# A fourth pair of each batch row by seven products, in a kernel of gated experts and an adapted linear layer on one core

## The reference, cut to what matters

```python
# layer 0, x is (8, 512, 256): 8 batch rows of 512 tokens
w, sel = top_k(softmax(cond_8), 2)               # two experts for each batch row, weights normalised
for each expert e:
    acc += w_e * (gelu(x @ gate_e) * (x @ up_e)) @ down_e      # 256 -> 1024 -> 256
x = x + acc + (gelu(x @ shared_gate) * (x @ shared_up)) @ shared_down
# layer 1, a linear layer with a low-rank part that depends on the batch row
x = x + x @ W_base.T + b_base + 2 * sum_e cond_8[b, e] * (x @ A_e.T) @ B_e.T
```

## Time and profile before

| what | value |
|---|---|
| median of 3 runs | 800.66 us (800.28 to 801.05) |
| the profiled execution, its own time | 800.03 us |
| its span, first to last instruction | 798.2 us |
| what lies outside the span | 1.8 us |
| busy share of the span: PE, PEld, DVE, ACT, POOL | 99%, 85%, 85%, 59%, 36% |
| granted PE clock | 0.999 of full speed |
| one batch row of the second stage | 67.58 us |

### The profile page before, as it was taken

The page is one execution under the profiler, slowest core; times in us unless marked ns, Lnnn a source line. Parts: engine busy times, 40 slices in busy tenths (PEclk is TensorE's granted clock), DMA queues, the critical chain, the costliest instruction groups (busy, mean ns, idle before and its releaser), DMA issues.

```text
span 798.2 us, 13016 instructions
## 1 busy us (share of the span) xinstructions
PE 792.9 (99%) x4014; PEld 678.4 (85%) x4014; DVE 676.6 (85%) x874; ACT 470.1 (59%) x715; POOL 290.5 (36%) x266
## 2 busy tenths in 40 slices
PE   9999999999999999999999999999999999999998
PEld 7888888888888888889888889888888888898887
DVE  4886987987876898899789789988978988998986
ACT  6564564564654656576566566566656655656653
POOL 1440321321110662552255055344415615533420
PEclk9999999999999999999999999999999999999999
DMA  7340520302313442353353254335334323533300
GB/s 211 75 120 12 148 80 12 121 1 89 110 40 80 139 135 84 106 154 112 102 152 90 87 163 121 106 105 131 105 120 146 105 80 122 152 107 103 84 1 28
DMA packets 120143, 80.56 MB, mean 101 GB/s; under 512 B 62481, under 2 KB 115473, under 8 KB 120081
## 3 DMA queue, kind: packets, MB, share of 16 engines
q1 hardware_dynamic: 120080, 79.88, 34.2%
HBM read 67.28 MB, written 12.58 MB: 100 GB/s over the span
## 4 chain that ended last, share of the span: by engine, by line
PE 99%; DMA 1%; DVE 0%; ACT 0%; SPq 0%; DVEq 0%; issue 0%
PE ps_ring L736 62%; PE ps_acc L736 36%; DMA raw<-_L_cond_shared_gate_dram 1%; PE ps_acc L944 0%; PE ps_acc L964 0%; PE ps_ring L754 0%; DVE stage L1798 0%; PE ps_ring L758 0%; PE ps_ring L762 0%; PE ps_acc L850 0%; PE ps_ring L964 0%; ACT xc L1065 0%; PE ps_acc L990 0%; ACT wide L1065 0%; SPq L456 0%
## 5 line engine op out<-in xcount | busy, mean ns | idle before, releaser
L736 PE MATMUL ps_ring<-xc,wide 128*128 128x512 f32 (+1 forms) x2076 | 454.1, 367 | 0.0
L736 PEld LDWEIGHTS ps_ring<-xc,wide 128*128 128x128 f32 x2076 | 366.3, 188 | 65.5 <-issue 0.3
L1065 ACT CAST inner_hi<-post 128x512 fp32r<-128x512 f32 x192 | 117.9, 621 | 140.8 <-DVE post L1723 67.6
L1404 DVE TENSOR_TENSOR inner_lo<-post,inner_hi 128x512 fp32r<-128x512 f32 x192 | 162.1, 858 | 12.2 <-ACT inner_hi L1065 11.8
L736 PE MATMUL ps_acc<-inner_hi,wide 128*128 128x512 f32 x504 | 172.0, 390 | 0.0
L1068 ACT ACTIVATE post<-ps_ring 128x512 f32<-128x512 f32 (+1 forms) x132 | 73.3, 558 | 89.4 <-PE ps_ring L736 85.4
L736 PEld LDWEIGHTS ps_acc<-inner_hi,wide 128*128 128x128 f32 x504 | 94.7, 188 | 19.2
L695 POOL TENSOR_TENSOR post<-post 128x256 f32<-128x256 f32 x48 | 34.5, 741 | 187.7 <-DVE post L1671 187.7
L736 PE MATMUL ps_acc<-inner_lo,wide 128*128 128x512 f32 x252 | 98.3, 390 | 0.0
L1723 DVE SCALAR_TENSOR_TENSOR post<-post,coef_now,ps_ring 128x512 f32<-128x512 f32 x80 | 59.4, 742 | 30.7 <-PE ps_ring L736 25.4
L736 PE MATMUL ps_acc<-inner_hi,sh_dn 128*128 128x512 f32 x256 | 83.8, 389 | 0.0
(11 more groups left out here) (122 smaller groups left out, 863.0 us busy)
## 6 DMA issues: line engine op xcount, KB each, us to landing
raw<-n_L_cond_skill_gate_dram SPq DMA_DIRECT2D x32, 256.0 KB, 2.9
raw<-in_L_cond_skill_up_dram SPq DMA_DIRECT2D x32, 256.0 KB, 3.4
raw<-n_L_cond_skill_down_dram SPq DMA_DIRECT2D x32, 256.0 KB, 3.7
xbuf<-n_L_cond_skill_gate_dram SPq DMA_DIRECT2D x32, 256.0 KB, 2.9
xbuf<-in_L_cond_skill_up_dram SPq DMA_DIRECT2D x32, 256.0 KB, 3.3
xbuf<-n_L_cond_skill_down_dram SPq DMA_DIRECT2D x32, 256.0 KB, 3.7
xt_scratch<-xbuf SPq DMA_DIRECT2D x8, 512.0 KB, 3.2
sh_scratch<-stage SPq DMA_DIRECT2D x8, 512.0 KB, 2.8
```

The lines of the kernel that those rows point to most:

```text
L736: last = pe.matmul(dst, left_[a], right_[b], start=start and n == 0, stop=stop and n == len(PASSES) - 1, skip_group_check=adds)
L1065: return nc.scalar.copy(dst, src)
L1404: return V.tensor_tensor(dst, src, hi.bitcast(F32), ALU.subtract)
```

## The change

- `SEVEN` becomes [1, 3, 5, 7]; batch row 0 keeps 3, 5, 7 (`FIRST_SEVEN`). So step 2 of batch rows 1 to 7 is by seven products too, behind only steps 0 and 1.
- The splits move: DVE and ACT take pair 9 (the next row's pair 1) at step 14, pair 2 at step 1, pair 3 and, with layer 1, pair 4 at step 4, and nothing at steps 0 and 2. The sums of pair 1 are split at step 0, those of pair 3 at `L1_STEP`.
- `L1_STEP` goes from 3 to 4. `layer1_sum` and `layer1_hi` stay at step 1, `layer1_lo` comes behind DVE's seven-product work of step 2, `turn_output` stands at step 5 behind the multiplication.
- `FOLD_STEP` 9 to 8; DVE's addition for it from step 12 to 9, its splits from step 13 to 12; `bw` from step 5 to 0.
- The token sums of batch row b+1 go to a second place in `sh_dn` for odd rows and are split at step 13 of row b; before, at step 3 of row b+1.
- x1 is written over `base`. The transfer of `base` for row b therefore waits for `x1_ready` (x1 split) instead of `x1_done`.
- POOL's order in a later row was: sums of pair 3, base plus x, `ex_c22`, sums of pair 5, token sums, `ex_c22`, sums of pair 7, `ex_c22`. It becomes the list in the diff.

```diff
-    L1_STEP = 3
+    L1_STEP = 4
-    FOLD_STEP = 9
-    W_EFF_STEP = 12
+    FOLD_STEP = 8
+    W_EFF_STEP = 9
+    W_EFF_LO_STEP = 12
     X_STEP = 8
+    T_STEP = 13
-    SEVEN = [3, 5, 7]
+    SEVEN = [1, 3, 5, 7]
+    FIRST_SEVEN = SEVEN[1:]
...
-        def sums_x(hl):
-            return xc[1][:, hl * 1024:(hl + 1) * 1024]
+        def sums_x(par, hl):
+
+            if par == 0:
+                return xc[1][:, hl * 1024:(hl + 1) * 1024]
+            return sh_dn[:, 2048 + hl * 1024:2048 + (hl + 1) * 1024]
...
-        x1 = post[:, 0:2 * S]
+
+        x1 = base
...
-        SPLIT_FIRST = {0: 2, 2: 3, 5: 4, 6: 5, 9: 6, 10: 7, 13: 8}
-        SPLIT_LATER = {0: 1, 2: 2, 5: 4, 6: 5, 9: 6, 10: 7, 13: 8}
-        SUMS_FIRST = {4: 0, 8: 1, 12: 2}
-        SUMS_LATER = {8: 1, 12: 2}
+        SPLIT_FIRST = {0: 2, 2: 3, 5: 4, 6: 5, 9: 6, 10: 7, 13: 8, 14: 9}
+        SPLIT_LATER = {1: 2, 4: 3, 6: 5, 9: 6, 10: 7, 13: 8, 14: 9}
+        SUMS_FIRST = {4: 1, 8: 2, 12: 3}
+        SUMS_LATER = {0: 0, 8: 2, 12: 3}
...
-                    sp.wait_ge(x1_done, b * 2)
+                    sp.wait_ge(x1_ready, b)
                     sp.wait_ge(sh_stored, 16 * B)
                     sp.dma_start(base, sh_dram[b]).then_inc(base_landed, 16)
...
+            def row(b, first, last):
+                if first:
+
+                    pool.wait_ge(sh_stored, 16 * B)
+                    sums_of_x(0)
+                    sums_of_weights(b, 1)
+                    row_sum(b)
+                    ex_c22(b, 1)
+                    sums_of_weights(b, 2)
+                else:
+                    sums_of_weights(b, 1)
+                    ex_c22(b, 0)
+                    row_sum(b)
+                    sums_of_weights(b, 2)
+                    ex_c22(b, 1)
                 if not last:
 
                     if not first:
                         pool.wait_ge(out_landed, b * 128)
                     pool.wait_ge(ex_t_ready, b + 1)
                     sums_of_x(b + 1)
-                ex_c22(b, 1)
-                sums_of_weights(b, 2)
+                sums_of_weights(b, 3)
                 ex_c22(b, 2)
+                if not last:
+                    sums_of_weights(b + 1, 0)
+                ex_c22(b, 3)
...
                         if k % 2 == 0:
-                            seven_products(b, par, k, SEVEN.index(k // 2))
-                            down(b, k - 2)
-                            down(b, k - 1)
+                            seven_products(b, par, k, SEVEN.index(k // 2), first)
+                            if k == 2:
+
+                                pe.wait_ge(x1_done, b * 2)
+                            down(b, k - 2, first)
+                            down(b, k - 1, first)
...
                     if k == L1_STEP and not first:
-                        split_pair(SEVEN[0])
-                        split_sums_w(b, 0)
-                    if k == L1_STEP + 1 and not first:
+                        split_sums_w(b, 1)
+                        split_pair(4)
                         add_bias(b - 1)
...
                             ex_seven(b, par, k, SEVEN.index(k // 2))
                             if k in split_at:
                                 split_pair(split_at[k])
+                            if k == 2:
+                                layer1_lo(b - 1)
...
-                    if k == 1 and not first:
-                        layer1_lo(b - 1)
                     if first and k == 1:
                         acc1_to_stage(Q - 1)
                     if k == L1_STEP and not first:
-                        split_pair(SEVEN[0])
-                        split_sums_w(b, 0)
-                    if k == L1_STEP + 1 and not first:
-                        turn_output(b - 1)
+                        split_sums_w(b, 1)
+                        split_pair(4)
                     if k == CONST_STEP and first:
                         layer1_constants()
+                    if k == T_STEP and not last:
+                        split_sums_x(b + 1, 1 - par)
```

More of the change, by code:

```diff
@@ L379, in cond_resid_kernel, with sevens_of, seventh, whole @@
         LAST_PARTS = [(c, slice(h * S // 2, (h + 1) * S // 2)) for c in range(2) for h in range(2)]
-        SPLIT_FIRST = {0: 2, 2: 3, 5: 4, 6: 5, 9: 6, 10: 7, 13: 8}
-        SPLIT_LATER = {0: 1, 2: 2, 5: 4, 6: 5, 9: 6, 10: 7, 13: 8}
-        SUMS_FIRST = {4: 0, 8: 1, 12: 2}
-        SUMS_LATER = {8: 1, 12: 2}
[L387 to L397, removed]
+        SPLIT_FIRST = {0: 2, 2: 3, 5: 4, 6: 5, 9: 6, 10: 7, 13: 8, 14: 9}
+        SPLIT_LATER = {1: 2, 4: 3, 6: 5, 9: 6, 10: 7, 13: 8, 14: 9}
+        SUMS_FIRST = {4: 1, 8: 2, 12: 3}
+        SUMS_LATER = {0: 0, 8: 2, 12: 3}
+        def sevens_of(first):
+            return FIRST_SEVEN if first else SEVEN
+        def seventh(b, k, first):
+            return sum(2 * pr < k for pr in sevens_of(first)) + (0 if first else b * NS - 1)
+        def whole(b, k, first):
+            now = k - 2 * sum(2 * pr < k for pr in sevens_of(first))
+            return now if first else b * (K - 2 * NS) + 2 + now
+        def seven_no(b, n_s):
+            return b * NS + n_s - 1
         block = ctx.enter_context(nc.Block())
@@ L696, in ex_c22, with row_sum @@
                 last.then_inc(ex_c22_done, 1)
[L698 to L706, removed]
+            def row_sum(b):
                 pool.wait_ge(base_landed, b * 16 + 16)
@@ L906, in seven_products, with down_chunk, down @@
                     last.then_inc(ex_product, 1)
[L908 to L913, removed]
+            def down_chunk(k, first):
+                return 1 - k % 2 if k // 2 in sevens_of(first) else k % 2
+            def down(b, k, first):
+                j, p = k % IC // 2, down_chunk(k, first)
                 pe.wait_ge(inner_ready, b * K + k + 1)
@@ L943, in one @@
                 def one(m, k, hl_w, hl_x):
-                    return pe.matmul(ps_acc[m][:], ex_dn(hl_w, k % IC // 2, down_chunk(k), m), inner_s[hl_x][:, k % 4, :],
+                    return pe.matmul(ps_acc[m][:], ex_dn(hl_w, k % IC // 2, down_chunk(k, False), m), inner_s[hl_x][:, k % 4, :],
                                      start=False, stop=k == K - 1 and (hl_w, hl_x) == (0, 1))
@@ L1015, in row @@
                     elif k >= 2:
-                        pe.wait_ge(gelu_done, whole(b, k - 1))
+                        pe.wait_ge(gelu_done, whole(b, k - 1, first))
                     elif k == 0:
@@ L1024, in row @@
                     elif k >= 2:
-                        pe.wait_ge(mul_done, whole(b, k - 1))
+                        pe.wait_ge(mul_done, whole(b, k - 1, first))
                     else:
@@ L1330, in row @@
                 for k in range(K):
-                    if k // 2 in SEVEN:
+                    if k // 2 in sevens_of(first):
                         if k % 2 == 0:
@@ L1365, in row @@
                             .then_inc(bw_hi, 1)
-                    act.wait_ge(mul_done, whole(b, k) + 1)
+                    act.wait_ge(mul_done, whole(b, k, first) + 1)
                     if k >= 4 or not first:
@@ L1709, in row @@
                                 split_pair(split_at[k])
+                            if k == 2:
+                                layer1_lo(b - 1)
                         continue
-                    dve.wait_ge(gelu_done, whole(b, k) + 1)
-                    dve.wait_ge(up_done, whole(b, k) + 1)
-                    if k % 2 == 0 and (k // 2 - 1 in SEVEN or (k == 0 and not first)):
+                    dve.wait_ge(gelu_done, whole(b, k, first) + 1)
+                    dve.wait_ge(up_done, whole(b, k, first) + 1)
+                    if k % 2 == 0 and (k // 2 - 1 in sevens_of(first) or (k == 0 and not first)):
                         dve.wait_ge(inner_ready, b * K + k)
@@ L1725, in row @@
                         .then_inc(mul_done, 1)
+                    if k == L1_STEP + 1 and not first:
+                        turn_output(b - 1)
                     if k == 1 and not first:
                         layer1_sum(b - 1)
-                    if k == (4 if first else 3):
-                        split_sums_x(b)
+                    if k == 4 and first:
+                        split_sums_x(0, 0)
                     if k in sums_at:
```

126 lines of the change are left out of this document (64 added, 62 removed).

## The result

The change makes the kernel slower: 809.88 us median (807.59 to 810.59, 6 runs) against 800.68 (800.28 to 801.59, 6 runs), a ratio of 1.011 with a 95% interval of 1.0099 to 1.012. Forecast were 804.1 us and a range up to 809.5. The profiled execution took 810.33 us, its span 808.5, 10.3 more than before.

What follows compares the result with a forecast made beforehand. PE was taken as the bound, busy 99% of the span, with DVE the first that may not keep up. Terms -2.7 + 1.5 + 1.7 + 3.0 = +3.5 on the profiled 800.03 give 803.5, median 804.1 us; range 797.9 to 809.5.

Steps and rivals of the forecast that it cites:

- The sign: Whole kernel: the change makes it slower, chance 0.50; same 0.18, faster 0.32.
- PE's saving, -2.7: Batch rows 1 to 7: one plain pair becomes a seven-product pair, saving 0.38 us each, 2.7 us in all.
- Later rows, +1.5 (0.25 a row): Six later rows: late DVE stalls PE 0.1 us at step 10 and 0.15 at step 14, 1.5 us in all.
- The limit of T + 3.48 for `ex_v`: Seven-product pairs: DVE's first sum must start within 3.48 us of T, the first product's start, or PE waits.
- T + 3.65: Step 14 of later rows: DVE's first sum starts 3.65 us after the first product's start, stalling PE 0.15 us.
- Batch row 0, +1.7: Step 10 of batch row 0: fold's addition, 0.6 us, and up to two POOL meetings, 1.1, stall PE 1.7 us.
- DVE's work, 65 us a row: Each later row: DVE busy 59.6 + 3.8 + 1.6 = 65 us of 67.2, fitting as a mean.
- the 0.72 of a whole POOL instruction: DVE meeting POOL: blocking by a whole POOL instruction, 0.72 us instead of 0.55, would lengthen chains 0.3 each, 3 us in all.
- The loop, +3.0: Two loop returns: DVE's new pass makes it late, stalling PE 1.5 us each around step 2, 3.0 us in all.
- With 2.6 more it is 5.7: Loop return: DVE, due 3.1 us into the next row, arrives at 5.7 after 2.6 us to begin its pass.
- The third rival: Steps 6 and 10: POOL becomes the bound, `ex_c22` 2 us late, stalls 1.2 us a row; +11.8, 812 us; chance 0.10.
- the bound between same and slower: Whole kernel: no change means within 0.2%, 1.6 us; slower means 802.3 to 809.5 us.

Runs made afterwards that it cites:

- place alone: Changed kernel with 120 always-fulfilled idle waits added to PE's list ahead of its loop, the loop's body unchanged: 804.59 us, 5.3 less than without them.
- the kernel before with the longer body: Kernel before the change with 64 always-fulfilled idle waits added to PE's loop body: 807.84 us; with 120 more waits ahead of the loop: 801.88 us.

## Why the prediction was wrong

The sign was right, with a chance of 0.5; the forecast was 5.8 us too low, and the time lies above the range. By its own terms:

- **PE's saving, -2.7: right.** 67.22 against 67.58 in rows without a stall, 0.36 each, and -0.33 in batch row 7.
- **Later rows, +1.5 (0.25 a row): too small.** Rows 1 to 6 are 0.12 us longer in all than before where they should be 6 x 0.36 = 2.16 shorter: 2.3 us of stalls, 0.38 a row. The limit of T + 3.48 for `ex_v` held: at T + 3.86 the stall was 0.37. Step 10 costs nothing there. At step 14 `ex_v` came at T + 3.86 and not T + 3.65: the inner split ahead of it met POOL as well (1.14 from start to start, 0.6 taken), and the pair's split took 1.93 where 2.2 was taken. Moving the token sums' split by a step took 2.6 us off.
- **Batch row 0, +1.7: right in place and size,** 1.7 at step 10, and 0.2 at step 14, which the forecast had not looked at there.
- **DVE's work, 65 us a row: too large,** 62.3 to 62.6 (59.56 before). It entered no term of the sum. A meeting with POOL cost DVE 0.26 to 0.60 us (2.01 for 1.75; 2.34 for 1.74) and in no split shown here the 0.72 of a whole POOL instruction.
- **The loop, +3.0: the step that failed, twice.** It reads: "With 2.6 more it is 5.7", that is, DVE's 2.6 us are put behind its last instruction. They were the part of the return that no work covered; the return is 2.8 us from DVE's branch on, in both kernels, and the split queued ahead of the branch covers most of it, so that DVE stood for 1.1 us. It costs 0.2 us at step 2, 0.5 for both. And it names DVE alone. PE's own loop has no term in the sum, its return was put at nothing without a word; it cost 4.23 + 4.18 = 8.4 us, shown by PE's branches (5.1 and 5.2 us where 0.2 is usual), the written-out loop (-7.5), by place alone (-5.3) and by the kernel before with idle waits (+7.3).

With the measured terms the sum is -2.5 (six rows and the last) + 2.3 + 1.9 + 8.4 = +10.1, and 0.16 ahead of the stage: the 10.3 of the span. DVE's 0.5 does not come on top, since PE is the later of the two at its own return; with PE's loop written out it shows, and 8.4 - 0.5 is the 7.9 by which that span is shorter (808.5 and 800.6). The third rival (POOL as the bound) gave 812, near the time, but by another mechanism: `ex_c22` of step 6 starts at 348.67, 0.14 us after the end of DVE's second sum, and no product waits there. That the sign came out right is partly luck: without the 8.4 us, which the forecast did not know of, the kernel is 1.9 us slower than before (802.41, PE's loop written out), near the bound between same and slower. More margin in DVE's chains would not have saved the forecast. The trace before the change had a sign of what could be lost, though no price: 21 packets of instructions for a loop that ran three times, and branches of 0.2 us, so its returns were free, and nothing in the forecast asked whether they would stay so.

## What to carry to other kernels

Ahead of a change that adds instructions to a loop, ask of each engine whether its return is free now. Afterwards look at how long its branch took and at its waits for "issue"; packets on the instruction queue without such a wait are no loss (33 with PE's loop written out), nor is "issue" in the chain that ended last (2% of the span in the changed kernel and in the written-out one alike). Let the loop written out, or idle waits ahead of it, tell a lost fetch from lost work. An idle time at a loop's return is no price: count from the branch, and see what the engine has queued ahead of it. When an engine is filled to 62.7 of 67.2 us with a deadline in every pair, where a piece stands can be worth more than how long it is, and what leaves one deadline can turn up at the next.

## What was not expected of the hardware

- A return of PE's loop that was not free cost 2.4 to 4.6 us here: a branch of 4.8 to 5.4 us, some 3 us of it beside queued matmuls, then a gap of 2.1 to 2.7 us, and with it, in four of the five traced, matmuls at a granted clock of 0.50 for some 3 us (1.7 us). Each moved 9 packets of 16 KB more.
- DVE's return is 2.8 us from the branch to the next instruction of its sequencer, in both kernels; beside a queued split of 1.75 us it cost the kernel 0.2.
- The same body misses or not by its place: 120 waits that do nothing made the kernel 5.3 us faster, and 6.0 us in the kernel before with the longer body (807.84 to 801.88).
- One and the same branch took 0.25 us at one return and 5.3 at the other (30 packets).
